# Zeroing the bucket ends of an edge sort with 7 writes of 32-row pieces in place of 13 writes of 16-row pieces

## The reference

```python
row = edge_index[0]                       # src, 206250 node numbers in random order
edge_aggr = jnp.zeros((n, HIDDEN), dtype=x.dtype).at[row].add(edge_features)
combined = jnp.concatenate([x, edge_aggr, global_expand], axis=-1) @ W_c + b_c
h = jax.nn.softplus(combined @ W1 + b1)
h = jax.nn.softplus(h @ W2 + b2)
# out = layernorm(x + h @ W3 + b3)
```

## Time and profile before

| | |
|---|---|
| median of the runs shown | 1762.06 us |
| the profiled execution | 1765.21 us |
| its span | 1763.4 us |
| mean granted TensorE clock over the span | 0.979 |
| the first gap write issued | 55.69 us from the span's start |
| first and last write of the bucket ends or spare tiles (L507) | 92.36 and 503.28 us |
| mean rate of the DMA engines | 234 GB/s |

### The profile page before, as it was taken

How to read it: one execution, slowest core, us unless ns; L and a number is a source line. 1 busy time by engine, 2 the same in 40 slices (tenths; PEclk the granted TensorE clock), 3 DMA queues, 4 the chain that set the end, 5 groups by cost and what they waited for, 6 DMA issues and landing times.

```text
span 1763.4 us, 60480 instructions
## 1 busy us (share of the span) xinstructions
PE 1674.5 (95%) x14853; PEld 1585.0 (90%) x14853; DVE 1329.0 (75%) x3881; ACT 1074.8 (61%) x3479; POOL 1178.2 (67%) x1482
## 2 busy tenths in 40 slices
PE   7887899999999999999999999999899999999985
PEld 4687899999989999999999999999899999999953
DVE  7774676777767777777777777777589999899956
ACT  1444455555555555555555555555488888888876
POOL 1565677777777777777777777777655555555535
PEclk9898999999999999999999999999899999999998
DMA  6378777777777777667766677777699999999922
GB/s 161 114 277 279 248 249 256 264 253 253 240 237 226 224 223 221 219 217 223 220 208 209 214 223 226 227 224 225 192 297 299 301 302 299 298 301 305 301 62 60
DMA packets 166151, 413.21 MB, mean 234 GB/s; under 512 B 28533, under 2 KB 43813, under 8 KB 163896
## 3 DMA queue, kind: packets, MB, share of 16 engines
q1 hardware_dynamic: 103824, 234.69, 42.9%
q0 software_dynamic: 54608, 174.58, 30.2%
q10 hardware_dynamic: 7689, 3.60, 1.2%
HBM read 234.52 MB, written 178.23 MB: 234 GB/s over the span
## 4 chain that ended last, share of the span: by engine, by line
PE 73%; DMA 12%; issue 4%; POOL 3%; DVE 2%; ACT 2%; POOLq 1%; ACTq 0%; SPq 0%; DVEq 0%
PE ps L1228 43%; PE ps L1300 22%; DMA buckets<-arena,index 6%; DMA arena<-in_feats 4%; PE ps L1186 2%; PE ps L1199 2%; PE ps L1239 2%; POOL buckets L522 1%; DMA buckets<-arena,direct_at 1%; DVE arena L875 1%; PE ps L1190 1%; ACT arena L1013 1%; PE ps L1335 1%; ACT reach L968 1%; POOL sums L564 0%
## 5 line engine op out<-in xcount | busy, mean ns | idle before, releaser
L1228 PE MATMUL ps<-arena 128*120 128x129 f32 x9084 | 1054.5, 275 | 2.8 <-DVE arena L803 2.8
L1228 PEld LDWEIGHTS ps<-arena 128*120 128x120 f32 x9084 | 1029.3, 185 | 5.4 <-DVE arena L803 4.0
L522 POOL DMA_INDIRECT buckets<-arena,index x757 | 786.9, 1040 | 260.6 <-issue 153.6
L803 DVE TENSOR_SCALAR arena<-slot_no,slot_f 128x360 f32<-128x360 f16 x1514 | 556.4, 420 | 260.4 <-PE ps L1228 231.1
L1013 ACT ACTIVATE arena<-ps 120x387 f32<-120x387 f32 x757 | 373.9, 494 | 374.3 <-PE ps L1228 317.9
L1300 PE MATMUL ps<-mark,members 128*128 128x128 f32 x3648 | 411.9, 276 | 8.1 <-ACT mark L1114 6.5
L1300 PEld LDWEIGHTS ps<-mark,members 128*128 128x128 f32 x3648 | 410.0, 192 | 10.1 <-issue 9.4
L847 DVE TENSOR_SCALAR mark<-node_no,members 128x128 f32<-128x128 f16 x1368 | 364.5, 334 | 52.0 <-DMA members<-buckets 42.2
L564 POOL TENSOR_TENSOR sums<-sums,staged 128x128 f32 x456 | 225.1, 494 | 198.1 <-ACT staged L1102 122.7
L968 ACT ACTIVATE reach<-block_no,arena 128x128 f16<-128x128 f16 x806 | 316.2, 394 | 0.7 <-PE ps L1239 0.7
L1108 ACT ACTIVATE apart<-node_no,members 128x128 f32<-128x128 f16 x456 | 181.2, 397 | 32.5 <-DMA members<-buckets 25.5
(11 more groups left out here) (169 smaller groups left out, 628.0 us busy)
## 6 DMA issues: line engine op xcount, KB each, us to landing
members<-buckets SPq DMA_DIRECT2D x456, 258.0 KB, 3.6
arena<-in_feats SPq DMA_DIRECT2D x201, 516.0 KB, 4.8
buckets<-arena,index POOLq DMA_INDIRECT x757
xn<-in_x ACTq DMA_DIRECT2D x1, 2800.0 KB
arena<-in_xT SPq DMA_DIRECT2D x11, 250.0 KB, 4.3
out_rows<-xn SPq DMA_DIRECT2D x11, 224.0 KB
buckets<-arena,direct_at POOLq DMA_INDIRECT x98
arena<-in_src SPq DMA_DIRECT2D x1, 805.5 KB
```

What stands on the lines that cost most here:

```text
L522: pool.indirect_dma_start(units, bass.IndirectOffsetOnAxis(ap=index[0:SLOTS, s, b:b + 1], axis=0), rows[0:SLOTS, o, :], None).then_inc(sca ...
L803: dve.tensor_scalar(perm[0:TP, b, t, :], slot_no[0:TP, :, :].rearrange("p r b -> p (r b)"), slot_f[0:TP, s, b * TPB + t:b * TPB + t + 1], ...
L1228: mm = pe.matmul(ps[0:SLOTS, MOVED + b, r * ROWF:(r + 1) * ROWF], perm[0:TP, b, t, r * SLOTS:(r + 1) * SLOTS], feat[0:TP, s, b * TPB + t, ...
```

## The change

The piece of a bucket-end write becomes 32 rows (PIECE = 8 * QR): 16 pieces cover a tile, a write takes 8 buckets, and 50 buckets take 7 writes. Fills: 4 + 7 = 11 bodies with a write instead of 17. END_GAP becomes 3 - 1 + 32 = 34 rows. The gap write of the last list is issued first, and the first scatter also waits for it. As engine instructions address partitions in groups of 32, and a bucket's pieces now lie on 16 partitions, VectorE first computes which of two buckets a partition belongs to and adds the two halves (17 instructions in place of 13). GpSimd gets two more iotas. The writes of the spare tiles are unchanged.

```diff
-    PIECE = 4 * QR
+    PIECE = 8 * QR
     PIECES = TROWS // PIECE
     AT_ONCE = P // PIECES
+    GROUPS = 4
     ENDS = -(-KS // AT_ONCE)
     FILLS = SPARES + ENDS
     END_GAP = GAP - 1 + PIECE
...
+            pool.iota(part_i[:, :], [[0, 1]], base=0, channel_multiplier=1).then_inc(iota_set, 1)
+            pool.iota(odd_end[:, :], [[0, KS // 2], [1, 2]], base=0, channel_multiplier=0,
+                      allow_small_or_imprecise_dtypes=True).then_inc(iota_set, 1)
...
-            for o in range(STREAMS):
+            for o in (STREAMS - 1, *range(STREAMS - 1)):
                 pool.indirect_dma_start(
                     units, bass.IndirectOffsetOnAxis(ap=gap_at[0:K, o:o + 1], axis=0),
                     zero_src[0:K, 0:(GAP if o < STREAMS - 1 else END_GAP) * ROWF], None).then_inc(scattered[o], 16)
...
                 if isinstance(i, int) and k < STREAMS:
+                    if k == 0:
+                        pool.wait_ge(scattered[STREAMS - 1], 16)
                     pool.wait_ge(scattered[o], 16)
...
-                for q in range(AT_ONCE):
-                    rows_ = slice(q * PIECES, (q + 1) * PIECES)
-                    dve.tensor_scalar(end_f[rows_, 0, 0:KS], tile_ends[rows_, 0, :], back_no[rows_, :],
-                                      float(q * PIECES * PIECE), ALU.add, ALU.add).then_inc(end_a, 1)
+                dve.wait_ge(iota_set, 11)
+                for part, shift in enumerate((4, 5)):
+                    dve.tensor_single_scalar(halves_i[:, part:part + 1], part_i[:, :], shift, ALU.logical_shift_right)\
+                       .then_inc(halves_cut, 1)
+                dve.wait_ge(halves_cut, 2)
+                dve.tensor_copy(halves_f[:, 0:2], halves_i[:, :]).then_inc(halves_cut, 1)
+                dve.wait_ge(halves_cut, 3)
+                dve.scalar_tensor_tensor(back_no[:, :], halves_f[:, 0:1], float(PIECES * PIECE), back_no[:, :],
+                                         ALU.mult, ALU.add).then_inc(end_parts, 1)
+                dve.scalar_tensor_tensor(halves_f[:, 2:3], halves_f[:, 1:2], -2.0, halves_f[:, 0:1],
+                                         ALU.mult, ALU.add).then_inc(end_parts, 1)
+                dve.wait_ge(end_parts, 2)
+                dve.tensor_scalar(odd_end[:, :], odd_end[:, :], halves_f[:, 2:3], None, ALU.is_equal).then_inc(end_parts, 1)
+                dve.tensor_scalar(end_f[:, 0, 0:KS], tile_ends[:, 0, :], back_no[:, :], None, ALU.add).then_inc(end_a, 1)
...
-                dve.tensor_scalar(end_f[:, 0, 0:KS], end_f[:, 0, 0:KS], junk_no[:, :], None, ALU.subtract).then_inc(end_a, 1)
-                dve.wait_ge(end_a, AT_ONCE + 1)
-                dve.tensor_tensor(end_f[:, 0, 0:KS], end_f[:, 0, 0:KS], end_f[:, 1, 0:KS], ALU.mult).then_inc(end_c, 1)
+                dve.scalar_tensor_tensor(end_f[:, 0, 0:KS], end_f[:, 0, 0:KS], junk_no[:, :], end_f[:, 1, 0:KS],
+                                         ALU.subtract, ALU.mult).then_inc(end_a, 1)
+                dve.wait_ge(end_a, 2)
+                dve.wait_ge(end_parts, 3)
+                dve.tensor_tensor(end_f[:, 0, 0:KS], end_f[:, 0, 0:KS], odd_end[:, :], ALU.mult).then_inc(end_c, 1)
                 dve.wait_ge(end_c, 1)
+                dve.tensor_reduce(end_of[:, :], end_f[:, 0, :].rearrange("p (j h) -> p j h", h=2), AX.X, ALU.add)\
+                   .then_inc(end_c, 1)
+                dve.wait_ge(end_c, 2)
...
-            act.wait_ge(fill_at_made, 1 + AT_ONCE)
+            act.wait_ge(fill_at_made, 1 + GROUPS)
```

More of the change, by code:

```diff
@@ L75, in gnn_bucketed_edge_sum_mlp_layernorm @@
     END_GAP = GAP - 1 + PIECE
-    assert FILLS <= BODIES and PIECES % 32 == 0
+    assert FILLS <= BODIES and 2 * PIECES * GROUPS == P and PIECES == 16
     FAR = (SPT * SPARES + 1) * TROWS
@@ L170, in gnn_bucketed_edge_sum_mlp_layernorm @@
         end_f = sb("end_f", [P, 2, ENDS * AT_ONCE])
+        odd_end = sb("odd_end", [P, KS])
+        part_i = sb("part_i", [P, 1], i32)
+        halves_i = sb("halves_i", [P, 2], i32)
+        halves_f = sb("halves_f", [P, 3])
+        end_of = sb("end_of", [P, ENDS * AT_ONCE // 2])
         fill_at = sb("fill_at", [P, FILLS])
@@ L279, in gnn_bucketed_edge_sum_mlp_layernorm @@
         fill_at_made = sem("fill_at_made")
+        halves_cut = sem("halves_cut")
+        end_parts = sem("end_parts")
         last_zeroed = sem("last_zeroed")
@@ L769, in zero_writes @@
                                   ALU.add, ALU.mult).then_inc(fill_at_made, 1)
-                for q in range(AT_ONCE):
-                    rows_ = slice(q * PIECES, (q + 1) * PIECES)
-                    dve.tensor_scalar(end_f[rows_, 0, 0:KS], tile_ends[rows_, 0, :], back_no[rows_, :],
-                                      float(q * PIECES * PIECE), ALU.add, ALU.add).then_inc(end_a, 1)
+                dve.wait_ge(iota_set, 11)
[12 more added lines that the diff above has]
+                dve.tensor_scalar(end_f[:, 0, 0:KS], tile_ends[:, 0, :], back_no[:, :], None, ALU.add).then_inc(end_a, 1)
                 dve.memset(end_f[:, 0, KS:ENDS * AT_ONCE], 0.0).then_inc(end_b, 1)
-                dve.wait_ge(end_a, AT_ONCE)
+                dve.wait_ge(end_a, 1)
                 dve.scalar_tensor_tensor(end_f[:, 1, 0:KS], tile_ends[:, 1, :], float(GAP - 1), end_f[:, 0, 0:KS],
@@ L778, in zero_writes @@
                 dve.wait_ge(end_b, 2)
-                dve.tensor_scalar(end_f[:, 0, 0:KS], end_f[:, 0, 0:KS], junk_no[:, :], None, ALU.subtract).then_inc(end_a, 1)
-                dve.wait_ge(end_a, AT_ONCE + 1)
-                dve.tensor_tensor(end_f[:, 0, 0:KS], end_f[:, 0, 0:KS], end_f[:, 1, 0:KS], ALU.mult).then_inc(end_c, 1)
-                dve.wait_ge(end_c, 1)
-                for q in range(AT_ONCE):
-                    rows_ = slice(q * PIECES, (q + 1) * PIECES)
+                dve.scalar_tensor_tensor(end_f[:, 0, 0:KS], end_f[:, 0, 0:KS], junk_no[:, :], end_f[:, 1, 0:KS],
[3 more added lines that the diff above has]
+                dve.tensor_tensor(end_f[:, 0, 0:KS], end_f[:, 0, 0:KS], odd_end[:, :], ALU.mult).then_inc(end_c, 1)
+                dve.wait_ge(end_c, 1)
+                dve.tensor_reduce(end_of[:, :], end_f[:, 0, :].rearrange("p (j h) -> p j h", h=2), AX.X, ALU.add)\
+                   .then_inc(end_c, 1)
+                dve.wait_ge(end_c, 2)
+                for q in range(GROUPS):
+                    rows_ = slice(q * P // GROUPS, (q + 1) * P // GROUPS)
                     dve.tensor_scalar(fill_at[rows_, SPARES:FILLS],
-                                      end_f[rows_, 0, :].rearrange("p (j q) -> p j q", q=AT_ONCE)[:, :, q],
+                                      end_of[rows_, :].rearrange("p (j q) -> p j q", q=GROUPS)[:, :, q],
                                       junk_no[rows_, :], float(RUNITS), ALU.add, ALU.mult).then_inc(fill_at_made, 1)
```

## The result

The changed kernel takes 1776.64 us, the median of 3 runs (1774.61 to 1777.65), against 1762.06 us before: a ratio of 1.0078, with a 95% interval of 1.0062 to 1.0094. It is slower by 0.8%. A later measurement of the same kernel beside new runs of the one before gave 1776.59 against 1764.83 us, 1.0070 (1.0056 to 1.0084). The profiled execution took 1774.61 us with a span of 1772.9 us, 9.5 us more than the span of before. The forecast was 1768.8 us, slower, within 1758.5 to 1778.5.

A forecast was written before the change was run, and what follows sets the result against it. TensorE was taken to set the time (chain 73% PE), sometimes waiting for transfers. Seven 32-row bodies (183.7 us) plus six without a write (137.7) replace 314.7 us: 6.7 us more, 1768.8 us, range 1758.5 to 1778.5.

The forecast's parts named there:

- The rule that TensorE waits 3.5 us less than ScalarE: In bodies behind a write, PSUM holds four batches, so TensorE waits 3.5 us less than ScalarE does for slot 3.
- the 32-row period: Bodies behind 32-row writes: 25.3 us if the clock holds, 27.5 us if it falls; seven sum to 183.7 us.
- The body with the clock held: A 32-row body at full clock: 22.84 us without waits, 2.0 us TensorE wait, 0.5 us other loss, 25.3 us.
- At 356 GB/s that is 3.0 us: A 32-row write moves 1.06 MB less than a 48-row one, so ScalarE waits 5.0 us for slot 3, not 7.95.
- what else a body loses: Loss in a body besides TensorE's wait: 0.5 us behind 16 rows, 2.7 us behind 48; 0.5 taken for 32.
- The clock: TensorE's granted clock falls in three of the seven 32-row bodies, at 2.2 us each.
- late scatters: Scatters landing late in 32-row bodies add up to 0.8 us to TensorE's 1.5 us wait; 2.0 us taken in all.
- the write itself costs, not its bytes: Rival on GpSimd's queue: 18 issues set the body, a 32-row write also costs 24.2 us; 1754.5 us, chance 0.12.
- alternation between queues: Skill page: engines alternate queues by packet, so a 32-row body costs no more than 16-row, sum 307.1 us; judged unsupported.
- Destinations: Four more VectorE instructions in zero_writes add 1.0 us, covered by the wait for slot 3: 0 taken, 1.0 if uncovered.
- The gap write: The 34-row gap write lands before the first scatter at 67.27 us and costs 0; at worst it holds it 11.4 us.
- The start: Before the bucket bodies: 0 taken; rival that the first scatter waits up to 11.4 us, 1780 us, chance 0.05.

The follow-up runs named there:

- after_again: The changed kernel measured again with no edit, for its spread: 1776.59 us against 1764.83 us for the kernel before, ratio 1.0070.
- mid32: The changed kernel with each fill issued behind the scatter of batch 9 of its body instead of behind the direct writes: 1745.55 us, ratio 0.9910.
- order34: The kernel before with only the gap part: last list's gap write 34 rows long and first, first scatter waiting for it: 1763.98 us, ratio 0.9999.

## Why the prediction came out as it did

**Right: direction, place and the wait.** The loss sits in the 32-row bodies, and the wait for slot 3 behind the write of zeros makes it; 48-row bodies and bodies without a write nearly kept their periods (29.6 and 22.87 us). The rule that TensorE waits 3.5 us less than ScalarE held exactly (5.99 and 2.47 us). The time lies near the upper end of the range; the loss was forecast as 6.7 us and measured as 14.6, later as 11.8 us.

**Too small: the 32-row period**, 26.2 us forecast on average (183.7 / 7), 27.12 measured. Seven times 0.88 is 6.1 us; less 0.5 us for six shorter bodies without a write this is the gap between the 6.7 us forecast and the 12.4 found. Two of its signs were missed with it: a release 13.5 to 14 us after the direct write (14.5) and a TensorE wait of at most 2.3 us (2.47). That it missed by no more is in part luck, since two errors have opposite signs:

- **The body with the clock held**, put at 25.3 us, is 26.8. ScalarE is released 14.5 us after the direct write, and where the clock holds 12.3 us follow to the next direct write (in after_again 26.15 - 13.87 and 26.40 - 14.13 us). "At 356 GB/s that is 3.0 us" is one part: taking 1.06 MB out of a 48-row write brought 7.95 - 5.99 = 2.0 us. The rows of the two queues fit this better: 1.19 + 0.20 MB in 3 us is 463 GB/s, by which 1.06 MB are an estimated 2.3 us, and the release moved from 16.8 to 14.5 us. The other part is "what else a body loses", put at 0.5 us: 26.8 - 22.84 - 2.47 = 1.5. It was taken from the 16-row bodies, as a loss of TensorE. But after a stall it is GpSimd that sets the rest of the body: it has eight scatters to issue before the next direct write, 307.00 to 318.01 us in the body shown.
- **The clock**, put at 3 x 2.2 us, "fall in three of the seven". It fell in all seven, for less: each of these bodies has a mean granted clock of 0.94, and they take 12.6 us from the release to the next direct write, 0.3 more than with the clock held. In after_again, bodies with the clock at 0.94 and 1.00:

```profile
265.90:293.17 27.27, 24.68 (x216) 23.74 (x215) 17.17 (x44) 12.93 (x41) 18.17 (x18) 0.94 0.77 262
...
375.02:401.42 26.40, 24.24 (x227) 23.30 (x226) 18.43 (x48) 13.86 (x43) 18.45 (x19) 1.00 0.80 271
```

They take 12.7 and 12.3 us behind a release at 14.57 and 14.13 us, and one body of that run at 0.88 takes 13.6. So one fall cost 0.3 to 0.4 us, a longer one 1.3 us. Most of the 2.2 us that the prediction gave to the halved clock was not the clock: behind the 48-row writes of the kernel before, 13.2 us follow the release, 0.9 more than with the clock held.

The added "late scatters" of up to 0.8 us, of which 0.5 were taken, did not come: 1.2 us in seven bodies. They hid part of the first error.

**Wrong about the bound: what a 16-row write costs.** I read its 1.26 us as a weaker form of the same stall, and wrote of the rival "the write itself costs, not its bytes" that three times the bytes for 7.0 us spoke against it. For the 16-row write that rival was right: 24.2 us is 18 issues of 1.34 us, and the run with a 66 KB write shows the issue alone to cost 1.41 us. So is the 22.95 us of a body without a write: 17 issues. GpSimd's groups of before over 524.45 to 1235.90 us:

```profile
L522 POOL DMA_INDIRECT buckets<-arena,index x465 | 487.2, 1048 | 142.5 <-issue 83.8 <-ACT arena L1013 49.3 <-ACT index L979 9.4
L533 POOL DMA_INDIRECT buckets<-arena,direct_at x63 | 63.8, 1013 | 19.2 <-issue 14.0 <-ACT arena L1013 4.9 <-ACT index L979 0.3
```

487.2 + 142.5 + 63.8 + 19.2 = 712.7 us for a stretch of 711.45. This was there to be read, and I took the chain's 73% PE for the bound instead. In the same terms a 32-row body is 18 issues and a stop: GpSimd is busy 127.0 us in the seven and idle 62.9, of which 126 x 0.30 us are the fixed distance, so it stands still for 3.6 us a body, and (127.0 + 37.8) / 7 + 3.6 = 27.1 us.

**The alternation between queues.** The prediction said of the alternation between queues that the trace does not bear it out. The conclusion, a later load behind a longer write, was right, the reading was not: the trace of before has the alternation, packet by packet, with packets of the write as long as a destination.

**The account in these terms.** Six writes fewer save six issues, 6 x 1.26 = 7.6 us. Seven writes of twice the size turn an issue hidden behind a nearly timely load into a stall: 7 x (27.12 - 24.21) = 20.4 us. 20.4 - 7.6 = 12.8 us, less 0.5 for the shorter bodies without a write: within 0.1 us of the 12.4 found. The same seven writes issued behind batch 9 of their body, seven issues earlier, keep the saving and lose most of the stall, which is why mid32 is faster than both.

**Smaller steps.** Destinations: 13 instructions took from 86.51 to 89.74 us, the 17 of the changed kernel 3.5 us, so 0.3 us more instead of 1.0; most of the added ones work on one or two columns and take 0.16 to 0.20 us. The gap write: forecast at 0 with 11.4 us as a rare end, measured 0. The start was put at 0 and is up to 1 us: the eight profiles of kernels with the whole change have the first direct write at 89.9 to 90.8 us, the five others at 88.8 to 90.0. The gap part alone does not do it (order34, 88.83 us), and the scatter of batch 7 is late already before the destinations are computed (79.20 against 78.16 us); the cause stays open.

## What to carry to other kernels

Before merging DMA writes, ask two questions of each: what its issue costs on the queue that issues it, and which transfer that somebody waits for is in flight beside or behind it. A merged write saves issues but is longer in the queues and, where its pieces grow, takes longer turns on the DMA engines; it belongs where no awaited load or buffer return comes within its duration. Count packets and MB by queue in a stretch in which both are in flight: it tells what share the awaited one gets. An engine whose idle time is only the fixed distance between its instructions is to be suspected as the bound, whatever share the chain of waits gives to another; here one more issue, of 66 KB, settled it.

## What the runs showed of the hardware

An indirect write on GpSimd costs 1.34 us of its queue from start to start, about 1.04 busy and 0.30 between, with 120 to 128 destinations and nearly whatever the length of each (24.4 us a body with 1-row pieces, 24.1 to 24.2 with 16-row pieces). The DMA engines took turns between GpSimd's and SyncE's queue packet by packet (48 to 48, 32 to 32), and a packet of a write of zeros was one whole destination, 8.3, 16.5 or 24.8 KB, against 4.1 KB for the load. A load issued 1.2 us behind a write with 16.5 KB to each of 128 destinations held ScalarE until 14.7 us after the direct write, whereas one issued 1.2 to 1.6 us ahead of it did so for 8.0 to 9.5 us. The granted clock fell to 1.2 GHz behind TensorE waits of 2.66 and, once, of 1.81 us (the body from 209.11 us of the changed kernel), while it stayed at 2.4 GHz behind one of 2.11 us (the body from 375.02 us of after_again) and behind most of the 16-row writes, with waits of up to 2.0 us.
